# Two transformer blocks with adaptive normalisation in one launch: experts, projections and copies of a hand-written plan are put into other steps

## The reference

```python
h = _layernorm(x) * (1 + ca) + sa
x = x + ga * attn(h)          # 16 heads of 16, causal: softmax(q k^T / 4 + mask) v, then o_proj
h = _layernorm(x) * (1 + cb) + sb
x = x + gb * ffn(h)           # below

xn = _layernorm(h) * ln_g + ln_b
att = softmax((xn @ wq) (xn @ wk)^T / sqrt(8))    # 32 heads of 8, not causal
o   = (att @ (xn @ wv)) @ wo + h
y   = gelu(o_half @ w1[e] + b1[e]) @ w2[e] + b2[e]   # two experts a batch, 256 rows each, 256 -> 1024 -> 256
```

## Time and profile before

| | |
|---|---|
| median of three runs | 1515.87 us |
| profiled execution, its own time | 1518.21 us |
| its span | 1516.3 us |
| TensorE busy | 1402.6 us, 93% of the span |
| VectorE busy | 1140.0 us, 75% |
| ScalarE busy | 993.4 us, 66% |
| GpSimd busy | 494.9 us, 33% |
| DMA | 204.96 MB, 135 GB/s mean |
| chain that ended last | PE 73%, DVE 12%, ACT 7%, issue 4%, DMA 2%, POOL 2% |

### The profile page before, as it was taken

The page is one execution under the profiler, slowest core; times in us unless marked ns, Lnnn a source line. Parts: engine busy times, 40 slices in busy tenths (PEclk is TensorE's granted clock), DMA queues, the critical chain, the costliest instruction groups (busy, mean ns, idle before and its releaser), DMA issues.

```text
span 1516.3 us, 29707 instructions
## 1 busy us (share of the span) xinstructions
PE 1402.6 (93%) x9537; PEld 597.5 (39%) x9537; DVE 1140.0 (75%) x2859; ACT 993.4 (66%) x2074; POOL 494.9 (33%) x1251
## 2 busy tenths in 40 slices
PE   6689898998999999999999999999999989998988
PEld 5234343332434344433434334343434323342437
DVE  6577888988686877869687887868788697868621
ACT  1045566777677676776668666776667766777772
POOL 4135553541341434315342243414343133302100
PEclk9599999999999999999999999999999999999999
DMA  6846554554365454726555463744546242524330
GB/s 196 230 112 182 114 150 115 156 170 102 93 199 129 137 130 115 216 76 181 129 148 132 135 176 93 204 126 137 141 111 193 77 127 61 175 76 133 100 115 15
DMA packets 193886, 204.96 MB, mean 135 GB/s; under 512 B 58432, under 2 KB 143744, under 8 KB 193736
## 3 DMA queue, kind: packets, MB, share of 16 engines
q1 hardware_dynamic: 188072, 199.08, 48.0%
q10 hardware_dynamic: 5664, 3.98, 1.0%
HBM read 123.99 MB, written 79.02 MB: 134 GB/s over the span
## 4 chain that ended last, share of the span: by engine, by line
PE 73%; DVE 12%; ACT 7%; issue 4%; DMA 2%; POOL 2%; SPq 1%; DVEq 0%; ACTq 0%; POOLq 0%
PE bank_out L1535 17%; PE bank_scores L1513 13%; PE bank_max L1491 9%; PE bank_side L1452 7%; PE bank_side L1632 6%; DVE max_column L1761 5%; PE bank_side L1465 4%; PE bank_max L1612 4%; ACT probs L1310 3%; PE bank_side L1573 2%; PE bank_side L1585 2%; PE bank_side L1612 2%; DVE bank_max L1758 2%; PE bank_scores L1612 2%; PE bank_side L1427 2%
## 5 line engine op out<-in xcount | busy, mean ns | idle before, releaser
L1310 ACT ACTIVATE probs<-bank_scores 128x512 f32<-128x512 f32 (+3 forms) x1536 | 752.5, 543 | 284.8 <-PE bank_scores L1513 279.8
L1761 DVE TENSOR_REDUCE max_column<-bank_max 128x1 f32<-128x512 f32 x1024 | 653.6, 683 | 105.0 <-PE bank_max L1491 100.1
L1535 PE MATMUL bank_out<-probs,v_tile 128*9 128x512 f32 (+4 forms) x3072 | 362.7, 544 | 5.7 <-issue 1.7
L1513 PE MATMUL bank_scores<-q_stack,k_stack 64*128 64x512 bf16 (+3 forms) x2048 | 315.6, 345 | 34.4 <-ACT probs L1310 29.6
L1491 PE MATMUL bank_max<-k_stack,q_stack 64*128 64x512 bf16 (+3 forms) x2048 | 313.0, 342 | 36.9 <-DVE max_column L1758 10.3
L1758 DVE CUSTOM_DVE_ANT_0 bank_max<-bank_max,causal 128x384 f32<-128x384 f32 (+3 forms) x512 | 241.7, 514 | 102.7 <-PE bank_max L1491 100.9
L1513 PEld LDWEIGHTS bank_scores<-q_stack,k_stack 64*128 64x128 bf16 x2048 | 80.7, 93 | 421.3 <-issue 412.9
L1157 POOL CAST max_parts<-max_row 128x32 bf16<-128x32 f32 x96 | 22.9, 239 | 447.9 <-DVE max_row L1774 447.5
L1491 PEld LDWEIGHTS bank_max<-k_stack,q_stack 64*128 64x128 bf16 x2048 | 104.2, 95 | 112.5 <-issue 73.7
L1632 PE MATMUL bank_side<-w_out,hidden_T 128*128 128x256 f32 x448 | 126.6, 405 | 0.0
L1535 PEld LDWEIGHTS bank_out<-probs,v_tile 128*9 128x9 f32 (+1 forms) x3072 | 47.5, 91 | 130.0 <-issue 93.6
(11 more groups left out here) (155 smaller groups left out, 1359.2 us busy)
## 6 DMA issues: line engine op xcount, KB each, us to landing
q_stack<-q_parts SPq DMA_DIRECT2D x124, 256.0 KB, 4.4
k_stack<-k_parts SPq DMA_DIRECT2D x124, 192.0 KB, 5.9
out_raw<-out_raw SPq DMA_DIRECT2D x74, 256.0 KB, 2.2
w_in<-in_L_ffn_w_dram SPq DMA_DIRECT2D x15, 1024.0 KB, 5.6
w_out<-in_L_ffn_w_dram SPq DMA_DIRECT2D x15, 1024.0 KB, 8.1
q_parts<-partsq SPq DMA_DIRECT2D x32, 384.0 KB, 2.9
k_parts<-partsk SPq DMA_DIRECT2D x32, 384.0 KB, 3.1
q_parts<-partsq SPq DMA_DIRECT2D x32, 256.0 KB, 3.1
```

What stands on the lines that cost most here:

```text
L1310: nc.scalar.activation(probs[s % 2][:, head_at(k), q0:S], region[bank][:, q0:S], ACT.Exp, scale=float(WIDTH[a]) ** -0.5).then_inc(drained[ ...
L1513: ins = pe.matmul(region[to][:, q0:S], k_stack[buf][rows, at, kt * P:(kt + 1) * P], q_stack[buf][rows, at, q0:S], start=(i == 0), stop=last)
L1535: ins = pe.matmul(outb[32 * k:32 * k + WIDTH[a] + 1, q0:S], v_tile[a][:, kt, g * GROUP + k, :], probs[s % 2][:, k, q0:S], start=(kt == 0), ...
L1761: v.tensor_reduce(dst, region[bank], AX_X, ALU.max).then_inc(drained[bank], 1)
```

## The change

It edits the plan's numbers, and makes two items divisible.

- `place_pass` (n = 1 to 5): the first expert's cluster goes from 93 to 123, three steps later, with `ffn_sum`, `attention_out`, `head_features` and the last `v` behind their new places, and its `expert_out` quarters after it. The first block's second layernorm (`layernorm_items(b, 1)`) now stands in steps 7 to 11 in place of under the cluster. `features_items(b, 2)` goes from 171/173 to 193/201, the eight `qk(1, b)` from one a step to 211, then two a step in causal steps 22 and 23, and `features_items(b, 1)` from 233/251 to 433/453. Behind the second cluster (303, not moved) the `expert_out` quarters start half a step sooner. `features_items(n+3, 0)` go from 393/403 to 383/393, and the `qk(0, n+3)` half a step to a step sooner.
- Start: the eight `qk(1, 0)` stand closer together and begin earlier, all ahead of the first score step; `v(1, 0)` and `stacks(1, 0)` follow sooner.
- First pass: `bias_part(0)` is in three pieces in steps 44 to 46 instead of step 49; `attention_out(1)` and the layernorms behind it up to a step later; `head_features(2, 0, 1)` from step 52 to 78; `stacks(1, 2)` three slots sooner; `keep_v(1)` in three pieces of 16, 12 and 4 heads from step 78 on instead of whole in step 81.

```diff
+KEPT_HEADS = ((0, 16), (16, 28), (28, 32))
...
     if n > 1:
-        place_units(plan, first, (3, 13, 61, 63), v_items(0, n + 2))
+        place_units(plan, first, (3, 13, 23, 83), v_items(0, n + 2))
...
-        place_units(plan, first, (33, 41, 43, 53), out_items(b))
+        place_units(plan, first, (43, 53, 63, 73), out_items(b))
...
-    place_cluster(plan, first, 93, e, 0, norm_under(b, 1))
...
+    place_units(plan, first, (71, 91, 93, 93, 93, 93, 93, 111, 113), layernorm_items(b, 1))
+    place_units(plan, first, (113, 121), [("ffn_input", b, 0), ("ffn_input", b, 1)])
+    place_cluster(plan, first, 123, e, 0, layernorm_items(b, 2)[:2])
...
-    place_units(plan, first, (181, 191, 201, 211, 221, 231, 241, 253), qk_items(1, b))
-    place_units(plan, first, (233, 251), features_items(b, 1))
-    place_units(plan, first, (263, 273, 283, 293), v_items(1, b))
+    place_units(plan, first, (211, 221, 223, 231, 233, 241, 253, 263), qk_items(1, b))
+    place_units(plan, first, (273, 283, 291, 293), v_items(1, b))
...
-        place_units(plan, first, (393, 403), features_items(n + 3, 0))
...
-    place_expert_out(plan, first, (313, 323, 333, 343), e, 1, 0)
-    place_expert_out(plan, first, (353, 363, 373, 383), e, 1, 1)
+        place_units(plan, first, (383, 393), features_items(n + 3, 0))
...
+    place_units(plan, first, (433, 453), features_items(b, 1))
+    place_expert_out(plan, first, (311, 313, 323, 333), e, 1, 0)
+    place_expert_out(plan, first, (343, 353, 363, 373), e, 1, 1)
...
-    place(plan, 15, [("head_features", 2, 0, 1)])
+    place(plan, 117, [("head_features", 2, 0, 1)])
...
-    place(plan, 85, [("stacks", 1, 2)])
+    place(plan, 82, [("stacks", 1, 2)])
...
-    place(plan, 130, [("keep_v", 1)])
+    place_at(plan, (116, 122, 130), [("keep_v", 1, piece) for piece in range(3)])
...
-    place_at(beside, (18, 20, 22, 24, 26), qk_items(0, 1)[:5])
+    place_at(beside, (14, 16, 18, 20, 22, 24, 25, 26), qk_items(0, 1))
...
-    place(beside, 18, [("stacks", 1, 0)])
+    place(beside, 10, [("stacks", 1, 0)])
...
+    place_at(beside, (175, 179, 183), [("bias_part", 0, piece) for piece in range(3)])
```

55 lines of the change are left out of this document (28 added, 27 removed).

## The result

The changed kernel takes 1507.75 us (median of 10 runs, 1501.95 to 1511.49) against 1515.91 for the kernel before, timed beside it (10 runs, 1513.9 to 1517.21): ratio 0.9938, 95% interval 0.9926 to 0.9950. It is faster by 8.2 us; 20.4 were forecast. The profiled execution is 1511.49 us, the slowest of the ten. Its span is 1509.6 us against 1516.3 before, so the two profiles differ by only 6.7 us.

The account below looks back on a forecast made before the run. PE was busy 93% of the span, its waits small and many, so no one bound to lift. Terms summed to -22.8, plus 2.4 for missed waits: -20.4, giving 1495.5 us for the median; 8-in-10 range 1486 to 1509.

Parts of the forecast that it names:

- second cluster's quarter: Behind the second cluster, an expert quarter fills PE's wait: 1.1 us less in passes 1 to 4, 0.7 in pass 5; -5.1.
- pass's end: Causal steps 38 to 41: earlier transposes remove waits at the next batch's first projection; -1.2 a pass, four passes, -4.8.
- `head_features`, causal steps, first cluster, `to_features`: Four terms of the pass: -1.8 for `head_features`, -2.5 for causal steps 17 to 25, +0.2 first cluster, -1.0 `to_features(6, 1)`.
- the start: Three more projections ahead of the first score step cost 4.5; less work, a maxima wait and slow clock go; -4.4.
- steps 50 to 57: First pass: `bias_part` moved to steps 44 to 46 no longer holds `attention_out` on DVE; -1.7 us.
- `stacks(1, 2)`: This stack load, three slots sooner, goes ahead of a maxima fetch, so PE's 1.87 us wait shrinks; -1.7.
- value copies: Value copies in three pieces take ACT 1.07 us either way; nothing, bounds -0.9 and +0.6.
- Both waits go: At a pass's end, the 0.81 us `act_T` delay and the projection's 0.83 us wait vanish with transposes in steps 38 and 39.
- third rival: The start gains nothing: half clock over all eight projections and a stack or maxima wait remains; 1500 us, chance 15%.
- Doubled projections: Causal steps 17 to 25: two projections a step use PE better, against new waits of 0.5 and 0.4; -0.5 a pass.
- second rival: The one bank "side" takes it back: causal stretch +1.0 a pass, pass's end brings half; 1505 us, chance 20%.
- First cluster: Second layernorm now in steps 9 to 11; step 12's maxima wait 0.25 to 0.7 for a bank; net +0.2.

Follow-up runs that it names:

- part with the weight later: Kernel before with only the first cluster's part of the pass changed, and the expert's second weight (1 MB) issued behind the maxima fetch: 1513.51 us, 0.9984.
- the second profile: The changed kernel run once more, unaltered, beside another kernel on the same chip: 1508.58 us, 0.9949 of the kernel before.
- three projections behind step 1: Five projections ahead, three behind step 1, stack load in step 3: 1510.42 on the kernel before, 1503.23 on the changed one, 1500.61 with the 1 MB weight later too.
- value sooner: The changed kernel with the first value projection of a pass one half step sooner: 1507.38 us, 0.9940 of the kernel before.
- not doubled: The changed kernel with the a=1 projections one a step, two value projections behind the second cluster and two output quarters doubled in non-causal steps: 1508.39 us, 0.9954.
- `keep_x`: The kernel of stack behind fetch with the copy of the expert's input one step sooner in every pass: 1509.47 us, 0.9958 of the kernel before.
- start undone: The changed kernel with the start as before, five projections ahead of the first score step and the first stack load in its old place: 1506.71 us, 0.9940.
- stack behind fetch: The kernel of start undone with the first stack load moved behind the fetch of the maxima: 1507.42 us, 0.9949 of the kernel before.
- first cluster: Kernel before with only the first cluster's part of the pass changed, second cluster's quarters and pass's end as before: 1521.73 us, 1.0036.
- eight only: Kernel before with eight projections ahead of the first score step in place of five, first stack load in its old place: 1523.44 us, 1.0053.
- the start alone: Kernel before with the whole new start and nothing else: 1515.71 us, 0.9999.

## Why the forecast was too large

The direction was right, and most waits that were to go went. The sizes were not: 20.4 us were forecast and 8.2 came. The steps, in us of the profiled executions:

| step of the forecast | forecast | measured | from |
|---|---|---|---|
| second cluster's quarter | -5.1 | -2.05 | alone, 5 x 0.41 |
| pass's end | -4.8 | -1.6 | added to it |
| `head_features`, causal steps, first cluster, `to_features` | -5.1 | -1.1 | part with the weight later, 5 passes |
| the start | -4.4 | 0 (-2.3 to +2.1 by the interval) | alone |
| steps 50 to 57 | -1.7 | -1.9 | -2.7 in steps 49 to 64, +0.8 in step 78 |
| `stacks(1, 2)` | -1.7 | -0.3 in the changed kernel's profile | below |
| value copies | 0 | -0.75 | step 82 |

**What failed first is the sentence "Both waits go" and the 1.1 a pass behind the second cluster: gaps were counted, and the slots left bare were not.** The waits went or shrank. But the number of PE's items is fixed, so an item moved into a gap leaves another half step bare. Moved alone, the quarters gain 1.06 and give some 0.65 back in slot 383. With the pass's end moved too, slot 383 is filled and the next pass's first step stands 0.6 more than before. I charged this for pass 5 alone and not for passes 1 to 4, although had the price: an item of 1.13 us adds only 0.33 to a bare step, so taking one away saves little. The two terms together were mis-sized by 6.2 us (-9.9 against -3.65), some 1.5 a pass: 0.6 is the bare half step, 0.39 the transposes in step 216, of which I had 0.2, and 0.3 to 0.5 was to come back in steps 220 and 221, where nothing came.

**The third row of the table.** In passes 3 and 4 these terms were right (-0.51 measured, -0.56 forecast), so most of what is missing is elsewhere. In pass 1 I had -1.9, and the part with the weight later is 0.5 slower there: the waits in steps 89 and 90 (1.24 for `ffn_sum`'s input, 0.87 for the cluster's) are gone, but the second halves of steps 88 and 89 are bare in their place, and from there to step 90 PE stands 2.1 us. Of the five waits of `head_features` that I counted, one (1238.49) is behind the last pass, where the change does nothing; it is there after the change too (1231.72, 0.36). In pass 5 the -1.0 for `to_features(6, 1)` came to nothing: the half steps that it moved into grew by 0.59 each, from 1.48 to 2.07 and from 1.92 to 2.51, so they had no room to spare.

**The start.** Its relief came mostly (-6.4 against -8.9 in steps 1 to 24); its price was +7.7 or, in the second profile, +5.0 against +4.5. The working was 3 x 3.0 - 2.5 - 2. The first projection starts at 58.46 against 59.78 before, so 1.3 sooner and not 2.5, and "the last runs at full clock" was wrong in the profiled execution, where all eight ran 2.08 us: 9.0 - 1.3 = 7.7. My third rival, a start that gains nothing, came true with half of its mechanism: the half clock did last over all eight, but no wait remained. The better question was what the three projections bought. It was the early stack load, and that is to be had without them, as the run with three projections behind step 1 shows (-5.1 us on the kernel before).

**Doubled projections.** Predicted waits of 0.5 and 0.4 came out at 0.49 and 0.39. Standing still in steps 193 to 202 went from 3.1 to 2.7 us; the forecast -0.5 a pass was right in size. The second rival, the side bank, had its mechanism right (waits for `rest` 9.7 us) and its place wrong: it was not what ate the gain. Its time, 1505, is nearer to the measured 1507.75 than my 1495.5, but not for its reason.

**First cluster.** The maxima at its head wait 0.25, the lower of my two ends. The Trainium skill (SBUF — State Buffer, Who interferes with whom) has VectorE and GpSimd block each other on shared ports. I had the last normalising piece at 0.55 a tile by it. Its two tiles take 0.73 us together (741.65), but POOL is idle beside them, so this piece doesn't test it. The trace of before agrees with the rule: four tiles take 2.21 us beside POOL's products (746.00) and 1.38 where POOL is idle (823.69).

**`stacks(1, 2)`** was right in about half of the executions. Of the ten profiles with the new place, five have a wait of 1.5 to 1.9 us for the fetch (the changed kernel twice, value sooner, not doubled, `keep_x`) and five have 0 to 0.3 (start undone, stack behind fetch, and the three with three projections behind step 1). The load of the stack has to wait for the last store of `k_parts`, and this 128 KB store landed after 4.5 us in all five profiles of the first kind, and after 3.2 or 3.3 in all five of the second. The changed kernel, then the one with three projections behind step 1:

```profile
k_parts<-partsk SPq DMA_DIRECT2D x1, 128.0 KB, 4.5
```

```profile
k_parts<-partsk SPq DMA_DIRECT2D x1, 128.0 KB, 3.2
```

Steps 65 to 80 take 52.2 us in the mean of the seven profiles with the old place in which the clock stays up, 52.7 in three of the first kind and 51.1 in the five of the second, and 0.8 of that is what step 78 pays. What decides when the store lands stays open.

## What to carry to other kernels

Where one engine is 97% busy and its side work is a fixed number of items, price a move by the slot it leaves as much as by the gap it fills: with the quarters moved alone, some 60% of what the gap gave was paid back in the slot left bare. When two transfers for one deadline share a queue, swapping them may only move the wait; look at what holds the first one, load earlier by moving what it depends on, and keep bulk loads behind the small, urgent ones. Edits that each look bad or good alone can do the opposite together when they act on one deadline, so time the pair as well.

## What the runs showed of the hardware that was not expected

The moment at which TensorE's clock rises from 1.2 to 2.4 GHz differs between executions of one kernel. In the changed kernel it was past 80 us in one profile (0.71 over 80 to 85) and near 75 us in the other:

```profile
75.00:80.00 5.00, 3.66 (x20) 1.78 (x20) 2.48 (x8) 1.49 (x5) 2.35 (x5) 1.00 0.47 155
```

so two of the projections took 1.13 us there instead of 2.07. By the granted clock of the profiles, TensorE was back at the full level between 69.6 and 75.9 us in the thirteen profiles with five projections ahead of step 1, and between 74.1 and 82.9 in the six with eight. The mean clock is 0.993 in the fastest run of the changed kernel (1501.95) and 0.984 in the slowest; the start alone has two runs at 0.993 (1510.83 and 1510.93), the others at 0.983 to 0.988 (1514.7 to 1519.88), and the fastest run of all (1497.34, value sooner) has 0.995. None of the 101 runs of the kernel before that were timed beside the experiments is above 0.989. An estimate from these means: 0.993 leaves some 21 us of a run at the lower level and 0.984 some 48, of which 41 are at the start in the profiled run (42 to 83 us). So in a few executions, all of them with eight projections ahead, the start spent much less time at the lower level; none of these was profiled.

The Trainium skill (TensorE: Matmul & The Clock Gate, What's actually happening) has activity open the gate; by it the denser start should have opened it sooner. PE was busier (7.14 of 10 us over 50 to 60, against 5.71), but the clock was at 0.50 until about 75 us or later in both, so this trace does not bear it out; in those few executions near 0.993 it may have. What decides between executions stays open.

A wait for a transfer does not always lower the clock. With a wait of 1.5 to 2.5 us in steps 72 and 73, the clock fell behind it in four profiles (first cluster, eight only, value sooner, `keep_x`), where steps 65 to 80 take 54.2 to 54.4 us, and stayed up in the others, where they take 51.9 to 52.8. Value sooner (wait 1.85), clock 0.66:

```profile
325.00:330.00 5.00, 4.55 (x22) 1.19 (x24) 2.40 (x5) 2.30 (x5) 2.45 (x7) 0.66 0.72 240
```

A small transfer can be slow to issue: the same three pieces of maxima took SyncE 1.70 us to issue, or 5.75 us with 1 MB issued 1.3 us ahead of them; with it 4.4 us ahead, 2.92.
